# A recommendation tower's CIN kernel: loads in another order, tile 0 gathered without waits, its products ahead of the weight additions, and the weight transposes behind its moments

## The reference

```python
e = stack([tbl_f[ids[:, f]] for f in range(26)], axis=1)        # 512 x 26 x 32
x1 = einsum('bik,bjk,hij->bhk', e, e, W1) + b1                   # H = 128
x2 = einsum('bik,bjk,hij->bhk', x1, e, W2) + b2
z = sum(concatenate([x1, x2], axis=1), axis=-1)                  # 512 x 256
h = concatenate([z, dense_ctx], axis=1)                          # 512 x 272
h = maximum(h @ W_top1 + b_top1, 0.0)                            # 512
h = maximum(h @ W_top2 + b_top2, 0.0)                            # 256
y = h @ W_top3                                                   # 512 x 1
```

## Time and profile before

| | |
|---|---|
| median of 3 runs | 177.65 us (177.57 to 177.9) |
| the profiled execution | 177.05 us, span 175.3 us |
| first fold | 11.31 us |
| first step of tile 0 | 49.73 us |
| first step of tile 1, 2, 3 | 84.87, 115.71, 146.54 us |
| last instruction of TensorE | 173.5 us |
| TensorE busy | 155.5 us (89%) |
| VectorE, ScalarE, GpSimd busy | 117.2, 74.5, 72.8 us |

### The profile page before, as it was taken

How to read it: one execution, slowest core, us unless ns; L and a number is a source line. 1 busy time by engine, 2 the same in 40 slices (tenths; PEclk the granted TensorE clock), 3 DMA queues, 4 the chain that set the end, 5 groups by cost and what they waited for, 6 DMA issues and landing times.

```text
span 175.3 us, 3331 instructions
## 1 busy us (share of the span) xinstructions
PE 155.5 (89%) x1273; PEld 147.0 (84%) x1273; DVE 117.2 (67%) x371; ACT 74.5 (43%) x188; POOL 72.8 (42%) x80
## 2 busy tenths in 40 slices
PE   6549999920999968999899999989999998999995
PEld 6449999910999967999799999979999997999993
DVE  5073748999979994699866669985666996432000
ACT  0205454800595543065555406455540645753022
POOL 2605065545665584545565455466555300000000
PEclk9978999995599999999999999999999999999999
DMA  3999910000000000001000000000000000000000
GB/s 98 410 399 397 351 46 12 9 8 11 11 11 10 9 11 8 11 9 15 11 8 15 8 9 14 13 11 8 15 8 9 14 0 0 6 0 0 4 0 0
DMA packets 4626, 8.71 MB, mean 50 GB/s; under 512 B 1761, under 2 KB 3425, under 8 KB 4354
## 3 DMA queue, kind: packets, MB, share of 16 engines
q1 hardware_dynamic: 1410, 3.63, 5.6%
q10 hardware_dynamic: 896, 3.68, 5.5%
q0 software_dynamic: 2304, 1.18, 4.8%
HBM read 8.49 MB, written 0.00 MB: 48 GB/s over the span
## 4 chain that ended last, share of the span: by engine, by line
PE 70%; DVE 15%; ACT 6%; DMA 5%; issue 2%; SPq 0%
PE bank L337 14%; DVE folded L680 8%; PE bank L345 8%; PE bank L283 8%; PE bank L350 7%; PE bank L354 7%; PE bank L299 6%; DMA w2t<-in_w2t_dram 5%; PE bank L358 5%; PE bank L377 2%; PE bank L375 2%; ACT diag L504 2%; PE bank L364 2%; PE bank L310 2%; ACT h L512 2%
## 5 line engine op out<-in xcount | busy, mean ns | idle before, releaser
L257 POOL DMA_INDIRECT rows<-in_tbl_dram,idx x72 | 72.0, 1000 | 64.1 <-DMA rows<-in_tbl_dram,idx 45.8
L337 PEld LDWEIGHTS bank<-diag,prod 128*128 128x128 f32 x256 | 30.5, 192 | 2.0 <-issue 1.5
L337 PE MATMUL bank<-diag,prod 128*128 128x108 f32 x256 | 31.4, 276 | 0.5 <-issue 0.2
L669 DVE COPY t<-bank 13x128 f32<-13x128 f32 (+1 forms) x64 | 16.8, 263 | 19.3 <-PE bank L345 18.6
L504 ACT ACTIVATE diag<-prod,quad 128x416 f32<-128x416 f32 (+1 forms) x32 | 17.5, 620 | 17.4 <-DVE prod L632 17.4
L485 ACT COPY t<-bank 128x432 f32<-128x432 f32 x32 | 15.0, 522 | 23.1 <-PE bank L337 23.1
L283 PE MATMUL bank<-small,onehot 128*128 128x256 f32 (+1 forms) x64 | 19.8, 412 | 1.4 <-DVE w1p L617 1.4
L617 DVE TENSOR_TENSOR w1p<-bank,chosen 128x320 f32<-128x320 f32 (+2 forms) x24 | 13.1, 547 | 10.9 <-PE bank L283 10.6
L345 PE MATMUL bank<-diag,prod 128*77 128x64 f32 x256 | 20.1, 230 | 0.0
L345 PEld LDWEIGHTS bank<-diag,prod 128*77 128x77 f32 x256 | 19.4, 149 | 0.0
L492 ACT COPY t<-bank 55x256 f32<-55x256 f32 (+2 forms) x48 | 14.1, 294 | 2.7 <-PE bank L345 2.3
(11 more groups left out here) (71 smaller groups left out, 197.3 us busy)
## 6 DMA issues: line engine op xcount, KB each, us to landing
idb<-in_idt_dram ACTq DMA_DIRECT2D x1, 1536.0 KB, 17.4
rows<-in_tbl_dram,idx POOLq DMA_INDIRECT x72, 2.4
small<-in_small_dram SPq DMA_DIRECT2D x1, 1120.0 KB, 12.1
wt<-in_W_top_dram SPq DMA_DIRECT2D x2, 512.0 KB, 17.5
w2t<-in_w2t_dram ACTq DMA_DIRECT2D x1, 832.0 KB, 8.1
w2t<-in_w2t_dram SPq DMA_DIRECT2D x1, 832.0 KB, 9.5
w1t<-in_w1t_dram ACTq DMA_DIRECT2D x1, 640.0 KB, 13.5
w1p<-in_w1p_dram SPq DMA_DIRECT2D x1, 521.0 KB, 7.4
```

What stands on the lines that cost most here:

```text
L257: pool.indirect_dma_start(rows[t][:, f, :], None, tables[f], bass.IndirectOffsetOnAxis(ap=idx[:, t, f:f + 1], axis=0)).then_inc(s_got[t][p ...
L337: mm = nc.tensor.matmul(m0[:, g % GBANK, :, 0:JW], prod[:, G, 0:P], diag[:, G, :, :], start=True, stop=True)
L669: ins = nc.vector.tensor_copy(t1[p0:p0 + HALF, GRAM + slot:GRAM + slot + nb, n], m1[64:64 + HALF, :].rearrange("p (n j) -> p j n", n=NSTEP ...
```

## The change

The loads: SP's queue brings all ids at once, `w1p`, `idb` of tile 0, `small`. ACT's queue brings `w2t` in three parts (6, 8 and 12 slices), then as before. GpSimd issues the 18 gathers of tile 0, and the first 5 of tile 1, without a wait; for later tiles four waits a tile are left. The lookups of tile 0 stand one to four groups later in the set-up.

VectorE's order: `low_terms` first pass, `half_b(0)`, second pass, `cross_a` and `cross_b` with the four `bands(0, s)` between the passes, `one_hot(1)` ahead of the last of them, and all picks of tile 1 after it. The vectors `b2x32` and `z1w` are made between the picks of tile 0 and `half_a(0)`.

TensorE: no lookup of tile 1 stands between tile 0's steps. All 12 groups of transposes come after them, through banks 6 and 7 by turns; the lookups of tile 1 stand after that, among `z2_low`, `z2_high`, `z1` and `layer1` of tile 0. `layer3(t - 1)` stands behind step 0 of tile t, and `copy_y` behind ScalarE's first take there. `spread(t + 1, 1)` is cut two and two round `relu2` instead of three and one.

```diff
@@ -77,7 +77,7 @@
-BURST = 3
+PAUSES = [(0, 8), (0, 12), (1, 20), (2, 25)]
@@ -99,6 +99,8 @@
+W2PARTS = [(0, 6), (6, 14), (14, 26)]
@@ -109,12 +111,11 @@
-HIGH = DONE["ctB"] + 4
-HOME = [RING[q % len(RING)] for q in range(DONE["ctB"])] + [0, 1, 2, 0] + [3, 4, 5, 7] + [0, 1, 2, 0]
+HOME = [RING[q % len(RING)] for q in range(DONE["ctB"])] + [6, 7, 6, 7] + [6, 7, 6, 7] + [6, 7, 6, 7]
-BEHIND = {6: 0, 8: 1, FOLDS - 1: 2, FOLDS: 3, FOLDS + 1: 4, FOLDS + 2: 5}
+BEHIND = {10: 0, 12: 1, FOLDS: 2, FOLDS + 1: 3, FOLDS + 2: 4, FOLDS + 3: 5}
@@ -228,9 +229,9 @@
-            sp.dma_start(idx[:, 0, :], io["ids"][:, 0, :]).then_inc(s_idx[0], 16)
+            sp.dma_start(idx[:], io["ids"]).then_inc(s_idx, 16)
             sp.dma_start(w1p[:], io["w1p"]).then_inc(s_w1p, 16)
-            sp.dma_start(w2t[:, 0:HALF, :], io["w2t"][:, 0:HALF, :]).then_inc(s_w2[0], 16)
+            sp.dma_start(idb[:, 0, :], on_all(io["idt"], 0, 1)).then_inc(s_idb[0], 16)
...
-                        if f > g0 and (f - g0) % BURST == 0:
-                            pool.wait_ge(s_got[t][part], 16 * (f - g0))
...
-                    pool.wait_ge(s_got[t][part], 16 * (f1 - g0))
+                        if t and (part, f) in PAUSES:
+                            if part == 2:
+                                pool.wait_ge(s_got[t][1], 16 * (PARTS[1][1] - PARTS[1][3]))
+                            pool.wait_ge(s_got[t][part], 16 * (f + 1 - g0))
@@ -399,51 +401,54 @@
-            pe.wait_ge(s_sf, FREE[DONE["ctB"]])
+            pe.wait_ge(s_sf, DONE["ctB"])
+            pe.wait_ge(s_turn[0], 1)
             for _ in range(FILL):
                 nc.tensor.matmul(bank[0][:, 0:P], ident[:], ident[:], start=True, stop=True)
-            for q in range(DONE["ctB"], DONE["v1"]):
-                make(q)
-            pe.wait_ge(s_sf, HIGH)
             pe.wait_ge(s_pad, 1)
             for t in range(TILES):
                 more = t < TILES - 1
                 for s in range(STEPS):
                     step(t, s)
-                    if more:
-                        if s == 0 and t == 0:
-                            pe.wait_ge(s_sf, DONE["v1"])
+                    if t and s == 0:
+                        layer3(t - 1)
+                    if t and more:
                         look_up(t + 1, s)
                 if t == 0:
-                    pe.wait_ge(s_e0, STEPS - 1)
-                    pe.wait_ge(s_e1, STEPS - 1)
-                    pe.wait_ge(s_eg, STEPS - 1)
-                    for q in range(DONE["v1"], len(SETUP)):
+                    for q in range(DONE["ctB"], len(SETUP)):
                         make(q)
-                    pe.wait_ge(s_sf, len(SETUP))
+                pe.wait_ge(s_e0, (t + 1) * STEPS)
+                if t == 0:
+                    look_up(1, 0)
+                    look_up(1, 1)
                     pe.wait_ge(s_vec, 32)
                     pe.wait_ge(s_wt, 48)
-                pe.wait_ge(s_e0, (t + 1) * STEPS)
                 z2_low(0, 6)
-                if more:
+                if t == 0:
+                    look_up(1, 2)
+                elif more:
                     look_up(t + 1, 4)
                 z2_low(6, HALF)
-                if more:
+                if t == 0:
+                    look_up(1, 3)
+                elif more:
                     look_up(t + 1, 5)
                 z2_high(t)
                 if t == 0:
+                    look_up(1, 4)
                     pe.wait_ge(s_z1w, 1)
                 pe.wait_ge(s_eg, (t + 1) * STEPS)
                 z1()
+                if t == 0:
+                    look_up(1, 5)
                 layer1(t)
                 layer2(t)
-                layer3(t)
+            layer3(TILES - 1)
...
                     ins.then_inc(s_e0, 1)
+                    if s == 0 and t:
+                        copy_y(t - 1)
...
                 if t < TILES - 1:
-                    spread(t + 1, 1, range(0, 3))
+                    spread(t + 1, 1, range(0, 2))
                 relu2(t)
                 if t < TILES - 1:
-                    spread(t + 1, 1, range(3, QUADS))
-                copy_y(t)
+                    spread(t + 1, 1, range(2, QUADS))
+            copy_y(TILES - 1)
...
+            dve.wait_ge(s_vec, 32)
+            nc.vector.tensor_scalar(b2x32[:], vec[:, 0:1], float(EMB), None, ALU.mult).then_inc(s_pad, 1)
+            dve.wait_ge(s_w1t, 16)
+            nc.vector.tensor_tensor(z1w[:], w1t[:, 0, :, :], w1t[:, 1, :, :], ALU.add).then_inc(s_z1w, 1)
             half_a(0)
             dve.wait_ge(s_sf, DONE["fold"])
             low = low_terms(folded)
             add(low, 0, False)
+            half_b(0)
             add(low, 1, True)
             dve.wait_ge(s_sf, DONE["ctA"])
             cross = cross_a(folded, ct[0])
             add(cross, 0, False)
+            bands(0, 0)
             add(cross, 1, True)
-            half_b(0)
             dve.wait_ge(s_sf, DONE["ctB"])
             cross = cross_b(folded, ct[1])
-            for t in range(TILES):
+            bands(0, 1)
+            add(cross, 0, False)
+            bands(0, 2)
+            add(cross, 1, True)
+            one_hot(1)
+            bands(0, 3)
+            for i in range(len(PICKS)):
+                pick(1, i)
+            half_a(1)
+            half_b(1)
+            for t in range(1, TILES):
```

More of the change, by code:

```diff
@@ L180, in arrive @@
         def arrive(t, pick):
-            return bank[6 + pick % 2] if t == 0 else bank[7]
-        s_idx = [sem(f"s_idx{i}") for i in range(2)]
+            return bank[6 + pick % 2] if t < 2 else bank[7]
+        s_idx = sem("s_idx")
         s_got = [[sem(f"s_got{t}_{part}") for part in range(3)] for t in range(TILES)]
@@ L187, in dlrm_tower @@
         s_idb = [sem(f"s_idb{i}") for i in range(2)]
-        s_w2 = [sem(f"s_w2{i}") for i in range(2)]
+        s_w2 = [sem(f"s_w2{i}") for i in range(len(W2PARTS))]
         s_iota = sem("s_iota")
@@ L526, in _ @@
             spread(0, 0)
-            for q in range(DONE["ctB"], HIGH):
-                take(q)
             spread(0, 1)
-            for q in range(HIGH, DONE["v1"]):
-                take(q)
             for t in range(TILES):
@@ L585, in _ @@
             linked()
[L586 to L590 removed]
+            dve.wait_ge(s_idx, 16)
             link(nc.vector.tensor_scalar(part_of[:], idx[:], CBITS, None, ALU.logical_shift_right))
@@ L593, in _ @@
             link(nc.vector.tensor_copy(partf[:], part_of[:]))
+            dve.wait_ge(s_w1p, 16)
+            nc.vector.tensor_tensor(w1s[:], w1p[:, 0, :], w1p[:, 1, :], ALU.add).then_inc(s_w1s, 1)
             linked()
@@ L708, in _ @@
                         pick(t + 1, s)
-                    if t == 0 and s < 2:
-                        add(cross, s, s == 1)
                 if more:
```

53 lines of the change are left out of this document (22 added, 31 removed).

## The result

The changed kernel took 206.92 us (206.35 to 207.75, 4 runs) against 177.78 us (177.57 to 178.49, 4 runs) for the kernel before on the same chip: a ratio of 1.1635, 95% interval 1.158 to 1.169. Forecast were 178.5 us and a range from 176.3 to 180.3. The sign was right; the size was wrong by 28 us.

A forecast was written before the change was run, and what follows sets the result against it. TensorE was taken as the bound from tile 1 on. Step 0 of tile 1 comes 1.2 us earlier, later tiles pay 2.0: +0.8 on 177.65 gives 178.5 us, range 176.3 to 180.3.

The forecast's parts named there:

- The step that failed: GpSimd's 18 gathers of tile 0, all issued by 27 us and wanted by half_b at 34, hide with 5 us to spare.
- First fold: TensorE's first fold in the set-up comes at 8.5 us instead of 11.31, because less data is loaded ahead of it.
- Rival 3: The loads don't come earlier: first fold at 9.5 us, all else 1.0 later, 179.5 us; chance 0.10.
- Last lookup of tile 0: TensorE ends its set-up folds, cross products and lookups at 23.8 us in place of 27.65, at full clock.
- Step 0 of tile 0: After VectorE's picks, half_a, low_terms and first half_b portion, it comes at 37.1 us, not 49.73; half clock costs nothing.
- Last lookup of tile 1, E: After tile 0's steps and transposes, TensorE's lookups among the z products end at 72.2 us; 72.66 before.
- The new wait: In tile 0's layer1, TensorE stands 3.7 us for ScalarE's copy of z2, queued behind a spread for tile 1.
- The clock in it: TensorE's clock falls during the layer1 stall, costing 1.5 us for layer1 and layer2; step 0 of tile 1 at 83.7.
- rival 1: The clock stays up in the layer1 stall: step 0 of tile 1 at 82.3, total 177.05 us; chance 0.26.
- Rival 2: TensorE's clock falls in the transposes ahead of tile 1's lookups, costing 1.9 us: 180.4 us; chance 0.10.
- The later tiles: Moved layer3 costs 0.45 us three times, the spread cut 0.34 twice: 2.0 us; copy_y costs nothing.
- Rival 4: Tile 0's late end costs less than thought, through better overlap and an earlier first fold: 176.4 us; chance 0.09.

The follow-up runs named there:

- e_after: The changed kernel unaltered, run again on another chip: 181.1 us, ratio 1.019 to the kernel before, no late results.
- d_b_unpaused: The kernel before with only the changed kernel's gather loop, which waits rarely: 204.5 and 212.5 us, against 177.4 for the kernel before on that chip.
- f_both: The changed kernel with all lookups of tile 1 ahead of tile 0's z products and the end of a tile as before: 200.6 us (once 211), ratio 1.118.
- p_early5: The changed kernel with gathers in waiting bursts of three and all lookups of tile 1 ahead of tile 0's z products: 188.6 us, ratio 1.051.
- c_tail: The changed kernel with at most three gathers in flight and layer3, copy_y and the spread cut at a tile's end as before: 249.2 us.
- d_tail: The same kernel as c_tail, unaltered, run on another chip: 249.6 us.
- d_slots3: The changed kernel with at most three gathers in flight, a_slots3 unaltered on another chip: 253.2 us.
- b_unpaused: The kernel before with only the changed kernel's gather loop, which waits rarely: 177.5 us, ratio 1.001.
- a_slots3: The changed kernel with a sliding limit of at most three gathers in flight, without draining between them: 185.0 us, ratio 1.043.
- a_pause_t0: The changed kernel with the later tiles' gather waits in tile 0 as well: 189.8 and 196.5 us, against 178.4 for the kernel before.
- e_spdma: The kernel before plus 90 small transfers on SyncE's queue, three in flight, into a buffer nobody reads: 177.7 us, ratio 1.001.

## Why the prediction was wrong

**The step that failed** is "the gathers of tile 0, 18 at 1.25 us ... They hide, with 5 us to spare". As transfers they did hide. What wasn't costed is what their rate does to the rest. The kernel before drains its queue every three gathers, the change takes that away, and the prediction asked only whether the rows would be there in time; it gave the edit neither a price nor a bound. In the result that is 24 of the 28 us: step 0 of tile 1 stands at 110.44 in after and at 86.30 in e_after. That the loop is the cause is shown by d_b_unpaused beside the kernel before, and for the new order, less strictly, by f_both beside p_early5; why it holds the engines up stays open (last section). No row of before showed the effect, so it could not have been priced, but a removed limit without a row is an unknown with two ends.

**The rest of the sum, on a chip without the hole.** e_after, timelines of TensorE and ScalarE and two stretches (busy time and count of all engines, or of PE alone, then clock):

```profile
8.72 7.09 PE L302 MATMUL bank<-w1s,w2t 128*128 128x183 f32 x44 [1.81 <-DVE w1s L596]
...
23.56 0.70 PE L286 MATMUL bank<-small,onehot 128*128 128x320 f32 x2
...
37.40 3.72 PE L339 MATMUL bank<-diag,prod 128*128 128x108 f32 x16 [4.70 <-DVE prod L831]
...
72.89 0.71 PE L286 MATMUL bank<-small,onehot 128*128 128x320 f32 x2
...
78.12 0.79 PE L377 MATMUL bank<-dctx,wt1c 16*128 16x128 f32 x2 [3.66 <-ACT z L544]
78.84 2.08 PE L379 MATMUL bank<-z,wt 128*128 128x128 f32 x8
...
86.30 2.01 PE L339 MATMUL bank<-diag,prod 128*128 128x108 f32 x16 [1.47 <-issue]
```

```profile
75.53 2.29 ACT L511 ACTIVATE diag<-prod,quad 128x416 f32<-128x416 f32 x4 [15.29 <-DVE prod L630]
```

```profile
50.00:60.00 10.00, 7.88 (x62) 5.75 (x61) 9.00 (x35) 8.05 (x21) 6.74 (x6) 1.00 0.06 11
...
79.00:80.00 1.00, 1.00 (x5) 0.50 0.13 32
```

- First fold: 8.5 forecast, bounds 7.9 to 9.5; 8.72 here, 7.3 to 7.9 in the other traces with the new loads. Here `w1s`, over at 8.66, decides it. Rival 3 (nothing earlier) is out.
- Last lookup of tile 0: over at 23.8 forecast, 24.26 measured. Full clock, as taken (1.00 from 20 to 25 us).
- Step 0 of tile 0: 37.1 forecast, 37.40 measured, and its products at half clock (3.72 us against 1.98, granted clock 0.50 from 37 to 42), as forecast, at no cost.
- Last lookup of tile 1, E: 72.2 forecast, 73.60 measured. The lookups started at 60.49 where 59.3 was forecast: the takes of the transposes were 1.2 us longer. This term was mis-sized; the other 0.2 us is the lookups and products of z.
- The new wait: E + 0.8 to E + 4.5 forecast; 74.46 to 78.12, which is E + 0.9 to E + 4.5. It stands behind the spread at 75.53, as said.
- The clock in it: fell, as taken, against rival 1 (0.50 in the stretch 79 to 80). From the first product of line 379 to step 0 it is 7.46 us here and 5.36 warm in p_early5, so the price is 2.1 us and not 1.5; and the warm way is E + 10.6 and not E + 10.0. Step 0 of tile 1 at E + 12.7, forecast E + 11.5.
- Rival 2, a clock that falls in the transposes: it stayed at 1.00 in the stretch 50 to 60, whose last 8.5 us hold transposes and their waits alone, and in the ten us behind it. The transposes filled 6.4 of those 8.5 us, not the 4.7 of 7.9 that the rival took. The rule of the Trainium skill (TensorE: Matmul & The Clock Gate, Part 4: PE-mode transpose), that transposes don't count like matmuls, isn't borne out here.
- The later tiles: 2.0 forecast, 3.2 measured (from step 0 of tile 1 to the end of the span 93.6 us in e_after, 90.4 before). In tiles 1 and 2, 0.7 of it lies between step 0 and step 1, where `layer3` now stands with 0.6, and 0.4 at the tile's end, the spread. In the last tile step 1 also waits 0.34 for `copy_y`, and the loss is 1.0; in after it waits so in tile 1 too (115.47, above). "Costs nothing" was wrong for that copy. c_tail and d_tail, without the moved tail, have 30.8 us a tile where d_slots3, with it, has 31.9 on the same chip as d_tail: the moved tail as a whole is the cause. Rival 4, a late end that costs less than forecast, is out.

Sum: 1.4 + 1.2 + 1.2 = 3.8 us over the forecast's 177.85 for a profiled execution, and e_after's took 181.6. Even there the median, 181.1, is 0.8 us above the range. The mechanisms were right, save for `copy_y`, and three sizes too small, each in the direction of an optimist: they were put together from durations in the kernel before, which don't hold what the new order adds between two instructions.

## What to carry to other kernels

When a change takes away a limit (a wait, a burst, a number of transfers in flight), ask what the limit protected besides its own data, and give its loss a bound even where no row shows it. When engines idle with no releaser in the trace, look for the engine that never idles in that stretch. Measure such a kernel on more than one chip before you believe either number: here one kernel took 185 us on one and 253 us on another.

## What the runs showed of the hardware

- On three chips of five, and on the result's, the other engines were held up beside a stream of indirect gathers 1.25 us apart: in d_slots3 TensorE and VectorE each started one instruction every 1.40 us, and in after TensorE's results came up to 20 us late to the engines that wait for them. On the other two chips three of the same programs ran without it: the changed kernel on E, b_unpaused and a_slots3 on B. In bursts of three in 5.2 us it was absent (before), or results were 1.6 us late once (p_early5).
- Where it happens, the traces have lost records: 1073 to 1243 of semaphore updates are left in the kernels without pauses, 1498 and 1600 in a_pause_t0 and p_early5, and 2078 to 2088 where nothing was late. The Trainium skill, NOTIFIC — the notification-queue block, section 7.1 Overflow: three behaviours, one of which stalls the engine, says that a full queue of such records, by its setting, either loses records or stalls the engine that feeds it. No run here shows which setting was on. The steps of 1.40 us and the losses could fit with it, but that recording has a part in the hole isn't shown: every timed run here was recorded, so no run tells whether the hole would be there without recording, and the one kernel with more records of another kind (e_spdma) fell on a chip without holes. What stays open is whether the small transfers, their signals or the records of both are the thing that jams, and what sets the chips apart.
